# Hats of three taps fetched in one set of transfers, with one ScalarE copy for the three and a ring of twelve

## The chip, the core and the metric

The kernel runs on one core of a Trainium2 chip (trn2). Its time is the device time of one execution in microseconds, the median of several; less is better. The five engines of the core each walk a list of instructions in order: TensorE (PE), VectorE (DVE), ScalarE (ACT), GpSimd (POOL) and SyncE (SP, which here only issues DMAs). They wait for one another by semaphores.

## What is computed

The input is 16 images of 64 channels and 16x16 pixels, in f32. Four layers follow one another:

```python
x = x + softmax(q @ k.T / 8) @ v                   # L0: attention over channels (64x64)
om = conv3x3(x, w_off) + b_off                     # L1: offsets (18) and mask (9) for each pixel
sampled[k] = bilinear(x, py[k], px[k]) * sigmoid(mask[k])      # k: 9 taps
x = relu(batchnorm(sum_k w_dcn[k] @ sampled[k] + b_dcn))
x = x + wp @ attention_over_pixels(q2, k2, v2)     # L2: 256x256 softmax for each image
y = depthwise3x3(layernorm(x))                     # L3
x = x + fuse @ sum_of_4_scans(conv5(y) * sigmoid(gate @ y))
x = x + ff2 @ (a * sigmoid(g)), [a, g] = ff1 @ layernorm(x)
```

## The kernel before

Two images stand side by side on the 128 partitions, so there are 8 pairs. Every engine walks its own list of PLAN (lines 56 to 127): an entry `step.n` is one step of pair n, and in PE's list `@m0` and the like name the PSUM bank (m0 to m2, or the double banks p0, p1 of `quad`). `turn` makes a PE step wait until the step that held its bank before is done. Nothing is ordered at run time: what stands behind a waiting instruction of an engine waits too.

**The hats.** Bilinear sampling is done by matmuls. The weight of a source pixel (y, x) for an output pixel is the product of two hats, one for each axis: max(0, 1 - |distance|), the hat of y times the mask. For each pair, `dist` (L847, DVE) gives the distances of each output pixel's position from the 16 rows and 16 columns, for 9 taps; `abs` (L678, ACT) and `hat` (L852, DVE) make the hats of them in the tile `hat` [128, 4, 18, 16]; `tanh` (L671, ACT) gives the mask, and `hat_y` (L860, DVE, scalar_tensor_tensor) multiplies (mask + 1) onto the y hats. PE transposes them in three groups of three taps, `tr0` to `tr2` (L467), ACT copies each out of PSUM (L686, 96 rows of 512), and `put` (L693, ACT's queue) writes them to `hat_rows` in HBM. A tap has 32 rows there, 16 of y and 16 of x, each of 2 KB (two images, 256 output pixels).

**The ring.** `get` (L333, L336, SP) reads a tap back with three DMAs: `xe`, 64 partitions of 2 KB (a row of x each, repeated for 4 runs), and two halves of `wt`, 64 partitions of 4 KB each (two rows of y, repeated for 16 columns). So one DMA moves 128 KB, two 256 KB. There is a ring of nine slots, RING = 9; a get waits until the sample nine taps back is done (`smp_mm`). ACT copies `xe` from partitions 0-63 to 64-127 (`d0` to `d8`, L712), DVE multiplies it into `wt` (`w0` to `w8`, L868, 128x1024), and PE samples (`s0` to `s8`, L497): four matmuls of the logical size 128x256 against `w_x`, all nine taps of a pair into the bank `cv`. `relu` (L719) takes the sum of nine taps out as x2. `w_x` are the images times the layer's weights (`wx0` to `wx2`, L482 and L703).

**Behind the samples.** qk2, logit, max (L875, L878), exp (L741), nrm (L888), et (L547, L750), av (L559), x3; then st1, ln1 (POOL: L1009 to L1018, five small steps; ACT: L757), dw (L762, L764, L910), y (L918), gs (gates and scans, L571 and L579, which need all four banks of quad), gate and scan (L774, L781), prod (L924), fuse (L589), x4 (L932), st2, ln2 (again POOL's five steps), ff (L601), u (L944), ff2 (L610), out (L951), store.

**Filler.** `warm` (L375) and `hot` (L381) are matmuls on a tile of zeros whose result nothing reads; one round is two matmuls of the program. WARM and HOT give the rounds of each entry. In the profile a matmul of f32 data appears as two; those of the filler as one.

## Time and profile before

| | us |
|---|---|
| median of 3 runs | 281.18 (280.73 to 282.88) |
| the profiled execution | 282.63 |
| its span in the profile | 280.8 |
| PE busy in it | 252.6 (90%) |
| DVE busy | 204.7 (73%) |
| ACT busy | 184.1 (66%) |
| POOL busy | 53.3 (19%) |
| DMA packets, bytes | 22881, 56.47 MB |

Times of instructions are from the profiled execution alone. An engine's share of busy time is an average over stages with different limits: the front, in which the first pairs' offsets are computed, the long middle in which 72 taps pass through the ring, and the tail behind the last sample, in which the last pairs' other layers end. "Idle before" tells how long an engine stood still ahead of a group of instructions and which instruction ended that. The DMA share can be a little above 1, as the durations of packets overlap.

### The profile page before, as it was taken

Reading aid. Unit: us, or ns where it says so; the run is one execution under the profiler, and the core shown is the slowest. Engines: PE = TensorE matmul, PEld = TensorE weight load, DVE = VectorE, ACT = ScalarE, POOL = GpSimd, SP = SyncE. Lnnn points to the kernel's source line nnn. Section 1 sums busy time; section 2 is a strip of 40 time slices with the busy share of each in tenths; the row PEclk is TensorE's granted clock in tenths of the full one; section 3 lists DMA queues with packets and bytes.
Section 4 is the critical chain, followed back from the end, with each engine's and each line's share of the span. In section 5 each row is a group of like instructions: output and inputs, shape, how many; then the busy total and the mean of one; then the engine's idle time right before and its main releaser. Section 6 shows DMA issues by size and latency. Waiting matters only on the chain.

```text
span 280.8 us, 7247 instructions
## 1 busy us (share of the span) xinstructions
PE 252.6 (90%) x2796; PEld 167.5 (60%) x2796; DVE 204.7 (73%) x353; ACT 184.1 (66%) x391; POOL 53.3 (19%) x99
## 2 busy tenths in 40 slices
...
GB/s 233 204 0 176 242 284 272 322 245 287 280 294 270 240 297 267 241 304 281 258 259 251 248 247 268 268 283 253 244 259 256 110 19 22 2 2 0 9 30 19
DMA packets 22881, 56.47 MB, mean 201 GB/s; under 512 B 4160, under 2 KB 6464, under 8 KB 22720
## 3 DMA queue, kind: packets, MB, share of 16 engines
...
## 4 chain that ended last, share of the span: by engine, by line
PE 51%; DVE 17%; ACT 13%; issue 9%; POOL 8%; ACTq 0%; DVEq 0%; POOLq 0%
PE ps_cv L497 11%; PE ps_quad L579 5%; PE ps_quad L482 5%; PE ps_m L444 5%; DVE sb_wt L868 5%; POOL sb_sc L1012 2%; PE ps_quad L571 2%; PE ps_m L467 2%; PE ps_quad L601 2%; ACT sb_xe L712 2%; PE ps_m L559 2%; DVE sb_b_max L875 2%; PE ps_m L511 2%; ACT sb_gates L774 2%; PE ps_quad L536 2%
## 5 line engine op out<-in xcount | busy, mean ns | idle before, releaser
L868 DVE TENSOR_TENSOR sb_wt<-sb_wt,sb_xe 128x1024 f32<-128x1024 f32 x72 | 87.9, 1233 | 11.7 <-ACT sb_xe L712 11.5
L497 PE MATMUL ps_cv<-sb_wt,sb_w_x 128*64 128x256 f32 x576 | 74.9, 388 | 5.3 <-DVE sb_wt L868 4.4
L497 PEld LDWEIGHTS ps_cv<-sb_wt,sb_w_x 128*64 128x64 f32 x576 | 40.2, 138 | 27.5 <-DVE sb_wt L868 7.9
L712 ACT ACTIVATE sb_xe<-sb_xe 64x512 f32<-64x512 f32 x72 | 44.8, 627 | 3.4 <-ACT sb_hats L686 1.6
L1009 POOL TENSOR_SCALAR sb_sc<-sb_mv 128x1 f32<-128x1 f32 x16 | 9.8, 612 | 116.6 <-DVE sb_mv L940 64.1
L910 DVE SCALAR_TENSOR_TENSOR sb_dw_acc<-sb_z_pad,sb_par,sb_dw_acc 128x256 f32<-128x256 f32 x56 | 23.0, 479 | 6.8 <-ACT sb_dw_acc L762 6.8
L482 PE MATMUL ps_quad<-sb_par,sb_x 64*128 64x256 f32 (+1 forms) x192 | 24.3, 378 | 0.8 <-ACT sb_w_x L703 0.6
L1002 POOL COPY sb_x<-sb_x_pad 128x256 f32<-128x256 f32 x8 | 6.3, 787 | 92.6 <-PE ps_quad L482 57.4
L774 ACT ACTIVATE sb_gates<-ps_quad,sb_gate_bh 128x512 f32<-128x512 f32 x16 | 10.1, 681 | 17.0 <-PE ps_quad L579 17.0
L703 ACT ACTIVATE sb_w_x<-ps_quad 128x1024 f32<-128x1024 f32 (+1 forms) x24 | 19.0, 807 | 3.0 <-PE ps_quad L482 1.8
L482 PEld LDWEIGHTS ps_quad<-sb_par,sb_x 64*128 64x128 f32 x192 | 16.7, 197 | 6.8 <-issue 5.7
L579 PE MATMUL ps_quad<-sb_y_pad,sb_par 32*64 32x256 f32 x640 | 20.4, 383 | 0.3 <-issue 0.3
L847 DVE TENSOR_TENSOR sb_dist<-ps_m,sb_grid 128x1152 f32<-128x1152 f32 x8 | 10.8, 1355 | 11.8 <-PE ps_m L455 11.8
L741 ACT ACTIVATE sb_b_exp<-ps_quad,sb_b_neg 128x256 f32<-128x256 f32 x32 | 14.8, 471 | 5.1 <-DVE sb_b_neg L878 4.8
L381 PE MATMUL ps_cv<-sb_idle 128*64 128x512 f16 x144 | 17.9, 396 | 0.0
L444 PE MATMUL ps_m<-sb_x_pad,sb_par 128*64 128x128 f32 x288 | 17.5, 272 | 0.4 <-DVE sb_x_pad L838 0.4
L579 PEld LDWEIGHTS ps_quad<-sb_y_pad,sb_par 32*64 32x64 f32 x640 | 14.0, 129 | 5.7 <-issue 3.4
L444 PEld LDWEIGHTS ps_m<-sb_x_pad,sb_par 128*64 128x64 f32 x288 | 16.4, 136 | 0.9 <-DVE sb_x_pad L838 0.4
L686 ACT ACTIVATE sb_hats<-ps_m 96x512 f32<-96x512 f32 x24 | 13.6, 590 | 5.2 <-PE ps_m L467 4.4
L467 PE MATMUL ps_m<-sb_par,sb_hat 128*96 128x128 f32 x96 | 13.9, 279 | 1.9 <-ACT sb_hats L686 1.4
L1012 POOL TENSOR_TENSOR sb_sc<-sb_sc,sb_half 128x1 f32<-128x1 f32 x16 | 14.4, 897 | 1.3
L467 PEld LDWEIGHTS ps_m<-sb_par,sb_hat 128*96 128x96 f32 x96 | 9.7, 126 | 7.7 <-issue 6.5
...
## 6 DMA issues: line engine op xcount, KB each, us to landing
sb_wt<-hat_rows SPq DMA_DIRECT2D x144, 256.0 KB, 10.3
...
```

Source lines behind the costliest of these rows:

```text
L381: nc.tensor.matmul(cv[columns_of(t), :], idle[:, columns_of(t)], idle[:, :], start=True, stop=True)
L444: mm = nc.tensor.matmul(ma[C * h:C * (h + 1), 0:P], par_sb[:, a + 2 * OM * t:a + 2 * OM * (t + 1)], x1_pad[n % 2][:, r:r + HALF_ROWS, t % ...
L467: mm = nc.tensor.transpose(ma[0:ROWS, at:at + P], hat[:, 2 * h + b, axes, :], ident)
L482: mm = nc.tensor.matmul(pair[:, 512 * b + PIX * h:512 * b + PIX * h + k], x1[n % 2][r, 2 * h:2 * (h + 1), :, :], par_sb[r, a:a + k], start ...
L497: mm = nc.tensor.matmul(cv[C * b:C * (b + 1), 0:PIX], w_x[n % 2][:, b, h, k, :], wt[slot(n, k)][:, h, PIX * b:PIX * (b + 1)], start=(k == ...
L579: mm = nc.tensor.matmul(quad[columns_of(d), 512 * i:512 * i + PIX], par_sb[r, a:a + C], rows, start=(j == 0), stop=(j == KS - 1))
L703: nc.scalar.activation(w_x[n % 2][:, :, :, t0:t1, :].rearrange("p b h t c -> p b h (t c)"), held(f"wx{c}", n)[:, :].rearrange("p (b h q) - ...
L712: nc.scalar.activation(xe[i][C:P, :], xe[i][0:C, :], ACT.Copy).then_inc(ev("dup_ok"), 1)
L774: last = nc.scalar.activation(gates[:, s, :, :], of_half(1, s), ACT.Tanh, bias=gate_bh[:, s:s + 1], scale=0.5)
L868: nc.vector.tensor_tensor(wt[i][:, :, :], wt[i][:, :, :], xe[i][:, :].unsqueeze(1).to_broadcast([P, HALVES, 2 * PIX]), ALU.mult)\
L910: nc.vector.scalar_tensor_tensor(out=sum_of, in0=dw_source(t), scalar=col("dw_w", t), in1=sum_of, op0=ALU.mult, op1=ALU.add).then_inc(ev(f ...
L1012: nc.gpsimd.tensor_tensor(scl[:, 1:2], scl[:, 0:1], half[:, :], ALU.pow).then_inc(ev(rstd_ok), 1)
```

## The change

1. The hats lie in another order: for each group of three taps, axis by axis, with the three taps innermost (`hat` is [128, 4, 3, 2, 48]). `abs` writes this order, the transposes read it without a step. In HBM a row of x or y now has its three taps side by side.
2. A get fetches a group: one DMA of 64 partitions x 6 KB (384 KB) and two of 64 x 12 KB (768 KB each). The ring has 4 slots of three taps; a get waits until all three samples of the group four back are done. The products of a group wait for both halves and for one ACT copy of 64x1536.
3. mask + 1 is computed by a new step `msk` on POOL, between `tanh` (ACT) and `hat_y` (DVE), which becomes a tensor_tensor.
4. The maximum of the softmax comes out negated (`negate=True`), the scale is put into q2; the step with -QK_SCALE is gone.
5. The two norms have four POOL steps in place of five; their gains with both signs are computed once, by four steps at the start.
6. Four buffers go (b_nrm, prod, ff_u, b_max), their results are written in place, with waits for the readers of the pair or two pairs before.
7. The lists of all engines are written anew, with other banks; HOT has 10 entries of 48 rounds in all (before 8 of 72), WARM 5 entries of 18 (before 6 of 18).

The core of the diff:

```diff
-RING = 9
+SLOTS = 4
...
     "pe": """
...
-        s4.8 v2.7@m1 et0.7@m2 s5.8 s6.8 s7.8 ff2.5@m2 s8.8 et1.7@m1 qk2.8@m2 av.7@m1 v2.8@m0 logit.8@p0 hot.1 et0.8@m1
-        gs.6@p0+p1 et1.8@m1 hot.2 av.8@m1 gs.7@p0+p1 fuse.6@m1 hot.3 fuse.7@m1 ff.6@p1 hot.4 gs.8@p0+p1 ff2.6@m1 hot.5
-        ff.7@p0 fuse.8@m1 hot.6 ff2.7@m1 hot.7 ff.8@p0 hot.8 ff2.8@m1
...
+        v2.7@m1 s1.8 gs.5@p0+p1 s2.8 fuse.4@m0 s3.8 s4.8 s5.8 ff.3@p0 logit.7@p1 s6.8 s7.8 s8.8 ff2.3@m0 fuse.5@m1
+        qk2.8@m2 et0.7@m0 ff.4@p1 logit.8@p0 et1.7@m0 v2.8@m1 av.7@m0 ff2.4@m1 hot.1 ff.5@p1 et0.8@m1 hot.2 et1.8@m0
+        hot.3 ff2.5@m1 av.8@m0 gs.6@p0+p1 hot.4 gs.7@p0+p1 fuse.6@m0 hot.5 gs.8@p0+p1 fuse.7@m0 hot.6 ff.6@p0 fuse.8@m0
+        hot.7 ff2.6@m1 ff.7@p0 hot.8 ff2.7@m0 hot.9 ff.8@p0 hot.10 ff2.8@m0
...
-HOT = {1: 15, 2: 5, 3: 11, 4: 9, 5: 10, 6: 4, 7: 10, 8: 8}
-WARM = {1: 5, 2: 3, 3: 3, 4: 2, 5: 3, 6: 2}
+HOT = {1: 2, 2: 2, 3: 1, 4: 10, 5: 6, 6: 6, 7: 3, 8: 8, 9: 2, 10: 8}
+WARM = {1: 5, 2: 3, 3: 3, 4: 2, 5: 5}
...
-        xe = [sb(f"xe{i}", [P, 2 * PIX]) for i in range(RING)]
-        wt = [sb(f"wt{i}", [P, HALVES, 2 * PIX]) for i in range(RING)]
+        xe = [sb(f"xe{i}", [P, OF_GROUP, 2 * PIX]) for i in range(SLOTS)]
+        wt = [sb(f"wt{i}", [P, HALVES, OF_GROUP, 2 * PIX]) for i in range(SLOTS)]
...
+            def get(g):
+                def step(n):
+                    sp.wait_ge(rows_out[n % 2][g], 16 * ((n + 1) // 2))
+                    wait_past(sp, ev("smp_mm"), OF_GROUP * (group(n, g) - SLOTS))
+                    i = slot(n, g)
+                    sp.dma_start(xe[i][0:C, :, :].rearrange("p t q -> p (t q)"),
+                                 rows[n - 1, g, ROWS // 2:ROWS, :].rearrange("(x t) q -> x (t q)", t=OF_GROUP).unsqueeze(1)
+                                 .to_broadcast([W, RUN, OF_GROUP * 2 * PIX])).then_inc(slot_x[i], 16)
                     for j in range(2):
...
+                        a = ROWS // 4 * j
+                        sp.dma_start(wt[i][C * j:C * (j + 1), :, :, :].rearrange("p h t q -> p (h t q)"),
+                                     rows[n - 1, g, a:a + ROWS // 4, :].rearrange("(y k) q -> y (k q)", y=RUN).unsqueeze(0)
+                                     .to_broadcast([W, RUN, HALVES * OF_GROUP * 2 * PIX])).then_inc(slot_in[i], 16)
...
+                nc.scalar.activation(hat[:, :, :, :, :].rearrange("p j g a (i t) -> p (j g) t (a i)", t=OF_GROUP),
+                                     dist[:, :, :, :].rearrange("p j (g t a) i -> p (j g) t (a i)", t=OF_GROUP, a=2), ACT.Abs)\
                     .then_inc(ev("abs_ok"), 1)
...
+            def dup(g):
+                def step(n):
+                    i = slot(n, g)
+                    act.wait_ge(slot_x[i], filled(n, g))
+                    nc.scalar.activation(xe[i][C:P, :, :], xe[i][0:C, :, :], ACT.Copy).then_inc(ev("dup_ok"), 1)
...
+                of_y = hat[:, :, :, 0, :].rearrange("p j g (i t) -> p (j g) i t", t=OF_GROUP)
+                mask = msk1[:, :, :].rearrange("p j (g t) -> p (j g) t", t=OF_GROUP).unsqueeze(2)                    .to_broadcast([P, 4 * GROUPS, H, OF_GROUP])
+                nc.vector.tensor_tensor(of_y, of_y, mask, ALU.mult)\
                     .then_inc(ev("hat_y_ok"), 1)
...
+                    g, t = divmod(k, OF_GROUP)
+                    i = slot(n, g)
+                    dve.wait_ge(slot_in[i], 2 * filled(n, g))
+                    dve.wait_ge(ev("dup_ok"), group(n, g))
+                    nc.vector.tensor_tensor(wt[i][:, :, t, :], wt[i][:, :, t, :],
+                                            xe[i][:, t, :].unsqueeze(1).to_broadcast([P, HALVES, 2 * PIX]), ALU.mult)                        .then_inc(ev("wt_ok"), 1)
...
-                dve.wait_ge(ev("max_ok"), n)
-                nc.vector.tensor_scalar(b_neg[n % 2][:, :], b_max[n % 2][:, :], -QK_SCALE, None, ALU.mult).then_inc(ev("neg_ok"), 1)
+                wait_past(dve, ev("exp_ok1"), n - 2)
+                nc.vector.tensor_reduce(b_neg[n % 2][:, :], held("logit", n)[:, :].rearrange("p (i j) -> p i j", j=PIX), AX_X, ALU.max,
+                                        negate=True).then_inc(ev("neg_ok"), 1)
...
+            def msk_step(n):
+                pool.wait_ge(ev("tanh_ok"), n)
+                wait_past(pool, ev("hat_y_ok"), n - 1)
+                nc.gpsimd.tensor_scalar(msk1[:, :, :], msk[:, :, :], 1.0, 1.0, ALU.add, ALU.mult).then_inc(ev("msk_ok"), 1)
```

## Rows read from the trace of the kernel before

**Rows 1.** The page, busy time (share of the span) and instructions of each engine

```profile
PE 252.6 (90%) x2796; PEld 167.5 (60%) x2796; DVE 204.7 (73%) x353; ACT 184.1 (66%) x391; POOL 53.3 (19%) x99
```

**Rows 2.** groups of instructions: the filler. busy us, mean ns | idle before us

```profile
L381 PE MATMUL ps_cv<-sb_idle 128*64 128x512 f16 x144 | 17.9, 396 | 0.0
...
L375 PE MATMUL ps_cv<-sb_idle 128*64 128x512 f16 x36 | 6.5, 450 | 1.2 <-DVE sb_idle L962 1.2
```

**Rows 3.** stretches: window, length, busy us of each engine, clock, DMA share, GB/s

```profile
5.00:10.00 5.00, 4.12 (x52) 2.79 (x48) 3.00 (x7) 0.73 (x4) 2.15 (x1) 1.00 1.02 376
30.00:219.00 189.00, 170.45 (x1880) 116.62 (x1876) 155.11 (x244) 138.06 (x287) 34.59 (x52) 0.98 1.04 267
219.00:231.20 12.20, 12.20 (x108) 7.72 (x106) 11.16 (x20) 9.77 (x22) 4.33 (x8) 1.00 0.14 46
231.20:280.80 49.60, 43.04 (x522) 24.12 (x520) 24.59 (x56) 21.51 (x44) 8.68 (x25) 0.96 0.04 12
```

**Rows 4.** timeline: start, duration of the first and last product and last sample

```profile
36.29 1.22 DVE L868 TENSOR_TENSOR sb_wt<-sb_wt,sb_xe 128x1024 f32<-128x1024 f32 x1
...
228.46 1.22 DVE L868 TENSOR_TENSOR sb_wt<-sb_wt,sb_xe 128x1024 f32<-128x1024 f32 x1
...
230.18 1.03 PE L497 MATMUL ps_cv<-sb_wt,sb_w_x 128*64 128x256 f32 x8
```

**Rows 5.** waits of SP's queue: us in total, times, longest

```profile
SPq L333 <- PE ps_cv L497: 27.6, 18, 3.1
SPq L304 <- PE ps_cv L497: 17.2, 10, 4.3
```

**Rows 6.** the page, DMA issues: KB each, median us to landing

```profile
sb_wt<-hat_rows SPq DMA_DIRECT2D x144, 256.0 KB, 10.3
```

**Rows 7.** waits of the compute engines: us in total, times, longest

```profile
DVE sb_wt L868 <- ACT sb_xe L712: 11.5, 11, 2.1
...
PEld ps_cv L497 <- DVE sb_wt L868: 7.9, 11, 2.4
```

**Rows 8.** groups of instructions: the copy, a longer ScalarE pass, the product

```profile
L868 DVE TENSOR_TENSOR sb_wt<-sb_wt,sb_xe 128x1024 f32<-128x1024 f32 x72 | 87.9, 1233 | 11.7 <-ACT sb_xe L712 11.5
...
L712 ACT ACTIVATE sb_xe<-sb_xe 64x512 f32<-64x512 f32 x72 | 44.8, 627 | 3.4 <-ACT sb_hats L686 1.6 <-issue 0.3
...
L678 ACT ACTIVATE sb_hat<-sb_dist 128x1152 f32<-128x1152 f32 x8 | 9.3, 1160 | 0.0
```

**Rows 9.** groups of instructions: the PE steps that move

```profile
L589 PE MATMUL ps_m<-sb_prod,sb_fuse_h 128*64 128x256 f32 x64 | 8.6, 390 | 0.6 <-DVE sb_prod L924 0.5
...
L601 PE MATMUL ps_quad<-sb_z,sb_par 64*128 64x256 f32 x64 | 9.7, 424 | 3.0 <-ACT sb_z L786 1.3 <-ACT sb_w_x L703 1.3 <-ACT sb_conv L781 0.4
...
L610 PE MATMUL ps_m<-sb_ff_u,sb_ff_h 128*64 128x256 f32 x32 | 5.1, 398 | 0.6 <-DVE sb_ff_u L944 0.6
```

**Rows 10.** timeline of the start, pair 1: abs, hat, first get

```profile
17.46 1.16 ACT L678 ACTIVATE sb_hat<-sb_dist 128x1152 f32<-128x1152 f32 x1
...
18.65 0.76 DVE L852 TENSOR_SCALAR sb_hat<-sb_hat 128x1152 f32<-128x1152 f32 x1 [1.32 <-ACT sb_hat L678]
...
23.67 0.61 SPq L333 DMA_DIRECT2D sb_xe<-hat_rows  x1
```

**Rows 11.** timeline of GpSimd: short steps, and one beside DVE's product

```profile
219.98 0.19 POOL L1016 TENSOR_TENSOR sb_sc<-sb_mv,sb_sc 128x1 f32<-128x1 f32 x1
220.25 0.19 POOL L1018 TENSOR_TENSOR sb_sc<-sb_par,sb_sc 128x1 f32<-128x1 f32 x1
226.89 1.10 POOL L1009 TENSOR_SCALAR sb_sc<-sb_mv 128x1 f32<-128x1 f32 x1 [6.45 <-DVE sb_mv L904]
```

**Rows 12.** timeline of the tail: negation, pair 8's y, its scans

```profile
237.19 0.17 DVE L878 TENSOR_SCALAR sb_b_neg<-sb_b_max 128x4 f32<-128x4 f32 x1
...
257.11 0.41 DVE L918 TENSOR_TENSOR sb_y_pad<-sb_dw_acc 128x256 f32<-128x256 f32 x1
...
261.11 0.74 PEld L571 LDWEIGHTS ps_quad<-sb_y_pad,sb_par 64*128 64x128 f32 x8 [0.41 <-issue]
```

More of the change, by code:

```diff
@@ L96 @@
-        ff.6 gate.8 ln2.7 scan.8 ff.7 ln2.8 ff.8
+        attn.1 at.1 mix.1 attn.2 attn.3 at.2 halve.1 off.1 prep.1 mix.2 abs.1 tanh.1 wx0.1 wx1.1 tr0.1 tr1.1 put0.1
+        tr2.1 wx0.2 put2.1 put1.1 off.2 at.3 attn.4 mix.3 tanh.2 abs.2 wx1.2 at.4 wx2.1 off.3 tr2.2 tr0.2 put0.2 put2.2
+        tanh.3 tr1.2 put1.2 mix.4 abs.3 d0.1 attn.5 off.4 d1.1 tr1.3 put1.3 at.5 tanh.4 tr0.3 put0.3 mix.5 d2.1 tr2.3
+        put2.3 abs.4 off.5 attn.6 relu.1 wx0.3 d0.2 q2.1 k2.1 wx2.2 wx1.3 tr2.4 put2.4 attn.7 tanh.5 d1.2 v2.1 exp0.1
@@ new lines @@
+        exp1.1 tr1.4 tr0.4 et0.1 wx2.3 put0.4 et1.1 put1.4 d2.2 at.6 abs.5 mix.6 at.7 ln1.1 dw.1 mix.7 d0.3 tr0.5 relu.2
+        put0.5 wx0.4 off.6 wx2.4 q2.2 k2.2 d1.3 v2.2 tanh.6 exp0.2 exp1.2 tr1.5 abs.6 put1.5 tr2.5 et0.2 d2.3 et1.2
+        put2.5 wx1.4 d0.4 tr2.6 ln1.2 relu.3 wx0.5 tr0.6 dw.2 tr1.6 q2.3 k2.3 v2.3 d1.4 put2.6 put0.6 put1.6 exp0.3
+        off.7 exp1.3 attn.8 d2.4 et1.3 et0.3 wx1.5 abs.7 tanh.7 at.8 d0.5 mix.8 relu.4 wx0.6 wx1.6 q2.4 k2.4 d1.5 gate.1
+        ln1.3 scan.1 dw.3 tr1.7 tr0.7 put0.7 tr2.7 d2.5 gate.2 put2.7 scan.2 put1.7 v2.4 off.8 d0.6 ln2.1 exp0.4 wx2.5
@@ L113 @@
-        x4.8 u.7 st2.8 out.7 u.8 out.8
+        qk.1 a_max.1 a_norm.1 qk.2 qk.3 a_max.2 a_max.3 a_norm.2 x1.1 a_norm.3 dist.1 qk.4 hat.1 hat_y.1 x1.2 a_max.4
+        dist.2 a_norm.4 x1.3 hat.2 hat_y.2 dist.3 qk.5 qk.6 hat.3 a_max.5 hat_y.3 x1.4 w0.1 a_norm.5 w1.1 qk.7 w2.1
+        dist.4 w3.1 w4.1 w5.1 x1.5 w6.1 w7.1 a_max.6 w8.1 a_norm.6 hat.4 qk.8 hat_y.4 dist.5 a_max.7 w0.2 w1.2 w2.2
+        max.1 a_norm.7 w3.2 w4.2 nrm0.1 nrm1.1 w5.2 x3.1 st1.1 w6.2 hat.5 w7.2 hat_y.5 w8.2 dw2.1 x1.6 dw4.1 w0.3 dw6.1
```

223 lines of the change are left out of this document (95 added, 128 removed).

## The prediction

> **What bounds the kernel now.** I read the busy times first. TensorE (PE) is busy 252.6 of 280.8 us, VectorE (DVE) 204.7, ScalarE (ACT) 184.1 [rows 1]. Part of PE's time is filler: 144 idle matmuls of "hot" (17.9 us) and 36 of "warm" (6.5 us) [rows 2], so the real PE work is 252.6 - 24.4 = 228.2 us, and about 52 us of the span are filler or gaps.
>
> Then I cut the span where the work changes its kind [rows 3]. From 30 to 219 us the DMA engines never rest (share 1.04) and PE is busy 170.45 of 189 us. From 219 on the gets are done, but sampling goes on: the last product of hats starts on DVE at 228.46 and the last sampling matmuls on PE at 230.18 [rows 4]. The last get had landed some 8 to 9 us earlier: from 219 to 231.2 the share is 0.14 of 12.2 us, 1.7 us of full work, so the stream ends near 220 [rows 3]. After 231.2 the tail of 49.6 us holds 43.04 us of PE, of which 17.9 are filler (all of hot stands behind sample 8.8 in the list): 25.1 us of real work [rows 2, 3]. So the end is set by two things: when sample 8.8 is done (231.2), and how long the chain of pair 8 is behind it.
>
> Is the middle bound by DMA? Its share says full, and SyncE (SP) waits 27.6 + 17.2 = 44.8 us in all for slots that sampling has not freed [rows 5]. A get lands a median of 10.3 us after its issue [rows 6], while a round of the ring of nine takes nine times (231.2 - 36.3) / 72 = 2.7 us, 24 us [rows 4]. So data lies ready for some 10 us before it is used, DMA is full but ahead, and the list of waits has no row of an engine that waited for a get to land. What the sampling does wait for is ACT's copy (11.5 us, 11 times), and PE's weight loads for DVE's product (7.9 us) [rows 7]. These are waits in an order written by hand: the engines (PE, DVE, ACT) are 90%, 82% and 73% busy in this stretch [rows 3], and each step stands behind others of its own engine.
>
> **The change, part by part.**
>
> *Transfers.* 216 gets become 72, of the same 46 MB (384 KB and two of 768 KB for each group). SP had 44.8 us to wait for slots [rows 5], so it was not the bound, and a third of the issues is worth nothing. The rate: gets with rows of 2 and 4 KB run at 267 GB/s at a share of 1.04; the loads at 5 to 10 us, with rows of 1 to 9.6 KB, at 376 at 1.02 [rows 3]. Rows of 6 and 12 KB are so bounded between 267 and 376. I take 267, since the gets read each row 16 times over and the loads do not; then a group lands 1.92 MB / 267 = 7.2 us after the one before. At 376 it would be 5.1. With the stream full as it is now, the last get lands near 219.5, or earlier at a better rate; behind it stand one copy of 1.48 (below), three products of 1.23 [rows 8] and the last sample of 1.03 [rows 4], so sampling can't end before 219.5 + 6.2 = 225.7 at the old rate.
>
> The Trainium skill (DMA: Bandwidth & Descriptors, "Why small descriptors are slow") says that joining descriptors is worth it only at 256 B and less. By that rule rows of 6 and 12 KB get no rate over those of 2 and 4 KB, the stream stays at 267 GB/s, and the rival of a faster stream (below) falls away. The trace does not decide it: 376 against 267 is also unique rows against repeated ones.
>
> *ScalarE.* 72 copies of 627 ns become 24. From 512 to 1152 elements a ScalarE pass grows by (1160 - 627) / 640 = 0.83 ns an element [rows 8], so 1536 elements cost 627 + 1024 x 0.83 = 1.48 us. 44.8 us become 35.5: 9.3 us less ACT. Little of it is on the path, as ACT is 73% busy; it serves the 11.5 us of DVE's waits, which I leave in the order's gain below [rows 7]. Against it, at the end, the last three products wait for a copy of 1.48 in place of 0.63: +0.85 us.
>
> *The order of work.* I compared the two lists on either side of sample 8.8. On PE these steps move from ahead of it to behind it: ff2.3, ff2.4, ff2.5, fuse.5, ff.4, ff.5, et0.7; none moves the other way. From the rows: ff2 5.1 / 8 = 0.64 each, fuse 8.6 / 8 = 1.08, ff 9.7 / 8 = 1.21 each [rows 9]; et0 is four matmuls of 128 columns, an estimate of 0.6 from half of fuse's. In sum 1.92 + 1.08 + 2.42 + 0.6 = 6.0 us. On DVE ten steps move likewise (prod.5, max.7, x4.5, st2.5, u.3 to u.5, out.3, out.4, nrm0.7), several microseconds, as prod.5 and max.7 alone each pass over as many elements as a product of 1.23 [rows 8]. Both engines that could hold sampling back are relieved, so sample 8.8 ends 6.0 us earlier, at 225.2, which the landing bound above (225.8) nearly allows. What moves behind must be taken up there: "hot" falls from 72 to 48 rounds, 48 matmuls of 17.9 / 144 = 0.124 us [rows 2] = 6.0 us less filler. The tail keeps its length and its filling. Bounds of this term: 0 (the middle keeps its end and only idles more) to -11.5 in place of -6.0, where the copy waits of rows 7 go too, all of them. I take -6.0.
>
> *The start.* The first gets go out at 23.67 [rows 10] behind the hats of pair 1. "hat_y" now waits for a new step on GpSimd (POOL), mask + 1, between ACT's tanh and DVE. Queued behind waiting hat_y on DVE are w's and x1 steps; queued behind msk on POOL are x1 (sampling weights) and the two norms. Its price is between 0.19 us, the shortest POOL row, and 1.10, the same kind beside a DVE product [rows 11]. In pair 1, abs comes before tanh: abs ends at 18.6, tanh at 18.8, msk at about 19.1, when DVE's own hat pass (18.65 to 19.41) still runs [rows 10]; so at most 0.2 is seen. In pairs 2 to 8 the hats are needed many microseconds later, hidden by the ring; without this cover it would be 8 x 0.19 to 8 x 1.10. I take +0.2. Four gain steps and one ScalarE scale at the start lie before 17 us beside PE work: nothing. PE's s0.1 comes behind mix.4, qk.7, x1.4 and off.4, the same work in another order: nothing.
>
> The first use: group 1 lands whole about 23.7 + 10.3 = 34.0 (7.2 of bytes, 3 of the way; the median landing of now, an estimate from rows 6), and w0.1 ran only at 36.29 [rows 4], with more ahead of it now: nothing.
>
> *Short steps of the last chain.* The softmax's negation (0.17 and a gap of 0.02 us) [rows 12] goes into the reduction; each norm loses one POOL step, 0.19 and 0.08 to the next [rows 11]: 0.19 + 2 x 0.27 = -0.73 us on pair 8. Elsewhere covered. Reusing buffers in place adds waits (exp on et of two pairs before, scan on fuse, ff on ff2 of the pair before); the PE list has each of those ahead of need, nothing, and up to 1.1 us (one fuse) where gs.7 precedes fuse.6.
>
> *The wait before the last scan.* Pair 8's y is written at 257.11 + 0.41 = 257.5, but gs.8 begins at 261.11 [rows 12], as ff.6 and the 18 idle matmuls of hot.4 stand ahead of it in PE's list. Now gs.8 has 12 idle matmuls before it and the PE work that moved back fills in. Between 0 and -3.6; I take -2.0.
>
> **Sum.** -6.0 + 0.85 + 0.2 - 0.73 - 2.0 = -7.7 us. Of the profiled execution (span 280.8, its time 282.63) this makes 273.1 and 274.9; that execution stood 1.45 above the median of 281.18, so the forecast is 281.18 - 7.7 = 273.5 us.
>
> **Rivals.**
>
> 1. *A faster stream.* Rows of 6 and 12 KB go at 350 GB/s or so and ACT's spare time takes DVE's waits away: of the 18.5 us in which PE idles from 30 to 219, a third (6 us) goes too. For it: 376 GB/s of the loads. Against: the data already waits 10 us. Time: 273.5 - 6 = 267.5.
>
> 2. *The middle does not shorten.* PE's gaps there belong to chains of softmax and norms over four engines, and work taken from PE leaves only wider gaps. For it: the waits of rows 7 are small and many, and none is a transfer. Against: PE is busy 12.2 of the last 12.2 us of sampling [rows 3]. Then -0.73 and 0.5 of the last wait remain: 280.
>
> 3. *Whole-group landing, the slower side.* A slot comes free only after its third sample and its data is of use only when all 1.92 MB are there, copied in one pass. With PE's order fixed, a stall at the first sample of each group pushes everything behind it. A landing takes some 10.3 us and a round of four groups 32, less 8 of use, so 13 us are spare, which speaks against it. For it: each put of hats must now be ready three taps sooner. If each of the 24 groups stalls 0.5 us: 281.2 - 7.7 + 12 = 285.5. It decides (slower than now) from 7.7 / 24 = 0.32 us a group.
>
> The Trainium skill (GPSIMD Engine Reference, "Key points") adds that GpSimd contends with VectorE instructions of two SBUF inputs, which each product is; that the new POOL step stretches from 0.19 to over 1 us is its case, and the trace agrees [rows 11].
>
> **Numbers.** Forecast 0.5 (its own range 270 to 278), rival 1 0.17, rival 2 0.20, rival 3 0.13. The range 267 to 282.5 reaches from rival 1 past rival 2. Three runs of the kernel before spread by 0.8%, so about 1% is what a measurement tells from no change. Faster by over 1% (below 278.4): rival 1 and nearly all of the forecast, 0.66; within 1%: rival 2 and edges, 0.20; slower 0.14.
>
> **What would show it.** Right: copies of 64x1536 at 1.48 us, ACT near 175 us busy; hot at 96 matmuls and 12 us; last sampling matmuls ending at 225 +/- 2; a tail of 46 to 48 us; gs.8 less than 2 us after y.8; gets at 267 to 300 GB/s. Wrong: sampling ending at 230 (rival 2), sampling rows of PE or DVE waiting for a get (rival 3), a share of DMA below 0.9 between 40 and 210 with an early end (rival 1).

## The result, and the profile after

The changed kernel takes 299.79 us (median of 4 runs, 296.0 to 304.55) against 281.06 (280.73 to 282.88, 4 runs). The ratio is 1.0531, with a 95% interval of 1.0451 to 1.0611: slower by 5%, where 273.5 us was forecast and 267 to 282.5 given as the range. The profiled execution took 302.85 us with a span of 301.1; it and one more of the four stood higher at a lower clock and are left out of the ratio, as such executions are from every ratio below, and the other two took 296.0 and 296.73, so of the 20.3 us that are followed below through the profiled span some 6 belong to that execution.

Busy times, and the issues of DMAs (KB each, median us from issue to landing) of the kernel after:

```profile
PE 257.0 (85%) x2748; PEld 169.6 (56%) x2748; DVE 202.2 (67%) x345; ACT 178.9 (59%) x344; POOL 50.9 (17%) x95
...
sb_wt<-hat_rows SPq DMA_DIRECT2D x48, 768.0 KB, 21.8
sb_xe<-hat_rows SPq DMA_DIRECT2D x24, 384.0 KB, 17.8
hat_rows<-sb_hats ACTq DMA_DIRECT2D x24, 192.0 KB, 12.8
```

No engine has much more to do than before [rows 1], and the span is 20.3 us longer: the engines wait. What for is in the list of waits (us in total, times, longest), first of the compute engines:

```profile
DVE sb_wt L869 <- DMA sb_wt<-hat_rows: 42.5, 18, 4.4
...
PE ps_cv L493 <- DVE sb_wt L869: 15.8, 13, 3.6
```

The row that did not exist before [rows 7] is now the longest of them for DVE: the product waits for the hats themselves, 42.5 us in all. Then of SP's queue:

```profile
SPq L301 <- PE ps_cv L493: 113.4, 17, 13.0
...
SPq L328 <- DMA hat_rows<-sb_hats: 55.2, 7, 16.9
```

SP waits 113.4 us for slots, against 44.8 before [rows 5], although the data then comes too late: the slots that sampling does not hold are issued already and not landed. A median landing of 21.8 us, where it was 10.3 [rows 6], is the same thing seen from the transfer. Puts wait among the long gets too (12.8 us, 7.8 before), and SP waits 55.2 us for them (16.9 before); low_first below has the loss without either. Stretches of the kernel after (length, busy us of each engine, clock, DMA share, GB/s):

```profile
35.00:238.00 203.00, 167.87 (x1696) 111.92 (x1697) 143.14 (x219) 123.19 (x223) 23.63 (x38) 0.92 1.02 239
...
255.00:301.00 46.00, 41.15 (x512) 23.81 (x508) 28.56 (x67) 25.69 (x52) 11.65 (x24) 0.99 0.06 19
```

Here is the loss. The DMA engines are as full as before (share 1.02) but move 239 GB/s where they moved 267 [rows 3]. Gets and puts are 47.2 + 4.7 = 51.9 MB, and 51.9 / 0.239 - 51.9 / 0.267 = 23 us. So much later the stream ends: DMA falls silent near 243, before near 220. The chain that ended last (start, us) shows it; gets of the y-hats are 38% of it, and the chain of the kernel before has none:

```profile
56.23 17.27 DMA sb_wt<-hat_rows
73.52 1.24 DVE sb_wt L869
...
85.03 24.74 DMA sb_wt<-hat_rows
...
117.15 29.11 DMA sb_wt<-hat_rows
...
160.51 22.33 DMA sb_wt<-hat_rows
...
197.97 20.83 DMA sb_wt<-hat_rows
218.82 1.23 DVE sb_wt L869
```

(PE's mean granted clock is 0.92 in this stretch, with PE busy for 83% of it, and was 0.98 with 90% [rows 3]. What the lower clock costs is not priced here.) The last product and the last sampling matmuls:

```profile
249.95 1.23 DVE L869 TENSOR_TENSOR sb_wt<-sb_wt,sb_xe 128x1024 f32<-128x1024 f32 x1
...
252.19 2.81 PE L493 MATMUL ps_cv<-sb_wt,sb_w_x 128*64 128x256 f32 x24
```

Sampling ends at 255.0 instead of 231.2 [rows 4], +23.8; the tail is 46.1 us instead of 49.6 [rows 3], -3.5; together +20.3, the whole difference of the spans. Two groups bear on the forecast: ScalarE's new copy came out as forecast, its abs did not.

```profile
L709 ACT ACTIVATE sb_xe<-sb_xe 64x1536 f32<-64x1536 f32 x24 | 35.6, 1483 | 8.5 <-DMA sb_xe<-hat_rows 8.0
...
L675 ACT ACTIVATE sb_hat<-sb_dist 128x1152 f32<-128x1152 f32 x8 | 14.4, 1801 | 4.5 <-DVE sb_dist L847 3.9
```

So the question for the experiments is: why do the same bytes, by fewer and larger transfers, move at 239 GB/s?

### The profile page after: what moved, and what is told of

Read it like the earlier page. It is cut to its first block, busy times and chain, and to the rows that moved or that the text cites. A ratio compares the mean times of both kernels' runs of the same rounds, so it can differ in the third digit from the quotient of the medians.

```text
span 301.1 us, 6980 instructions
## 1 busy us (share of the span) xinstructions
PE 257.0 (85%) x2748; PEld 169.6 (56%) x2748; DVE 202.2 (67%) x345; ACT 178.9 (59%) x344; POOL 50.9 (17%) x95
## 4 chain that ended last, share of the span: by engine, by line
DMA 44%; PE 36%; DVE 7%; ACT 5%; issue 3%; SPq 2%; POOL 2%; ACTq 0%; POOLq 0%; DVEq 0%
DMA sb_wt<-hat_rows 38%; PE ps_cv L493 8%; DMA hat_rows<-sb_hats 6%; PE ps_quad L575 6%; PE ps_quad L567 3%; DVE sb_wt L869 2%; PE ps_m L463 2%; PE ps_quad L597 2%; PE ps_quad L478 2%; PE ps_m L543 2%; PE ps_cv L372 2%; PE ps_m L441 1%; ACT sb_conv L780 1%; PE ps_m L555 1%; PE ps_m L387 1%
## 5 line engine op out<-in xcount | busy, mean ns | idle before, releaser
L869 DVE TENSOR_TENSOR sb_wt<-sb_wt,sb_xe 128x1024 f32<-128x1024 f32 x72 | 87.9, 1232 | 42.5 <-DMA sb_wt<-hat_rows 42.5
L493 PE MATMUL ps_cv<-sb_wt,sb_w_x 128*64 128x256 f32 x576 | 76.6, 401 | 17.9 <-DVE sb_wt L869 15.8
L493 PEld LDWEIGHTS ps_cv<-sb_wt,sb_w_x 128*64 128x64 f32 x576 | 41.5, 142 | 42.2 <-issue 15.7
L709 ACT ACTIVATE sb_xe<-sb_xe 64x1536 f32<-64x1536 f32 x24 | 35.6, 1483 | 8.5 <-DMA sb_xe<-hat_rows 8.0
L1022 POOL TENSOR_SCALAR sb_sc<-sb_mv 128x1 f32<-128x1 f32 x16 | 8.3, 522 | 119.9 <-DVE sb_mv L940 89.4
L910 DVE SCALAR_TENSOR_TENSOR sb_dw_acc<-sb_z_pad,sb_par,sb_dw_acc 128x256 f32<-128x256 f32 x56 | 24.3, 477 | 1.5 <-ACT sb_dw_acc L761 1.4
L700 ACT ACTIVATE sb_w_x<-ps_quad 128x1024 f32<-128x1024 f32 (+1 forms) x24 | 18.9, 808 | 1.5 <-PE ps_quad L478 1.0
L675 ACT ACTIVATE sb_hat<-sb_dist 128x1152 f32<-128x1152 f32 x8 | 14.4, 1801 | 4.5 <-DVE sb_dist L847 3.9
L463 PEld LDWEIGHTS ps_m<-sb_par,sb_hat 128*96 128x96 f32 x96 | 10.6, 133 | 11.1 <-issue 9.3
L1016 POOL TENSOR_SCALAR sb_msk<-sb_msk 128x36 f32<-128x36 f32 x8 | 3.6, 449 | 72.7 <-ACT sb_msk L668 72.7
L876 DVE TENSOR_REDUCE sb_b_neg<-ps_quad 128x4 f32<-128x1024 f32 x8 | 9.8, 1221 | 7.0 <-PE ps_quad L532 7.0
## 6 DMA issues: line engine op xcount, KB each, us to landing
sb_wt<-hat_rows SPq DMA_DIRECT2D x48, 768.0 KB, 21.8
hat_rows<-sb_hats ACTq DMA_DIRECT2D x24, 192.0 KB, 12.8
```

The source lines that it names most:

```text
L463: mm = nc.tensor.transpose(ma[0:ROWS, at:at + P], hat[:, 2 * h + b, g, :, :], ident)
L493: mm = nc.tensor.matmul(cv[C * b:C * (b + 1), 0:PIX], w_x[n % 2][:, b, h, k, :], wt[slot(n, k // OF_GROUP)][:, h, k % OF_GROUP, PIX * b:PI ...
L675: nc.scalar.activation(hat[:, :, :, :, :].rearrange("p j g a (i t) -> p (j g) t (a i)", t=OF_GROUP), dist[:, :, :, :].rearrange("p j (g t ...
L700: nc.scalar.activation(w_x[n % 2][:, :, :, t0:t1, :].rearrange("p b h t c -> p b h (t c)"), held(f"wx{c}", n)[:, :].rearrange("p (b h q) - ...
L709: nc.scalar.activation(xe[i][C:P, :, :], xe[i][0:C, :, :], ACT.Copy).then_inc(ev("dup_ok"), 1)
L869: nc.vector.tensor_tensor(wt[i][:, :, t, :], wt[i][:, :, t, :], xe[i][:, t, :].unsqueeze(1).to_broadcast([P, HALVES, 2 * PIX]), ALU.mult) ...
```

## The experiments

Fifteen kernels ran, two of them twice. The letters of theories are each text's own; A2 is the one that first stands in stream4. Where the computation is left out, the times say nothing of the kernel; only the GB/s of the stretches are read.

### Which part of the change: order_before, rows4k, tapgets

**order_before** keeps the change's transfers and takes the lists and filler of before.

```diff
-    (the changed PLAN, HOT and WARM)
+    (those of the kernel before; get and copy of a group where its first tap's stood, msk behind bn.1 and x1)
```

> The changed kernel with the lists and the filler of the kernel before (the copy of a group where its first tap's stood, the mask step put in behind the sampling copies of GpSimd). Theory A and B: still 295 or more, as the transfers are the new ones. Theory C (the new order is the fault): back to 281 to 285.

302.43 us, ratio 1.0752 (1.0702 to 1.0802). The loss is there with the old order. The y-hats land in 19.9 us, puts in 13.3.

**rows4k** keeps all of the changed kernel, its HBM layout and its one semaphore for a group, but cuts the three transfers into nine, with rows of 2 and 4 KB, and the y-hats for partitions 0 to 63 and 64 to 127 in turn.

```diff
-                    for j in range(2):
+                    for c in range(3):
+                        for j in range(2):
...
-                        sp.dma_start(wt[i][C * j:C * (j + 1), :, :, :].rearrange("p h t q -> p (h t q)"),
+                        sp.dma_start(wt[i][C * j:C * (j + 1), :, :, :].rearrange("p h t q -> p (h t q)")[:, 4 * PIX * c:4 * PIX * (c + 1)],
```

> The changed kernel, with each group's three DMAs cut into nine of 2 and 4 KB rows, same slots, same semaphores for the whole group. Theory A (row length sets the rate, and the rate the time): the stream returns to 260 GB/s or more, the puts of hats land in 8 us instead of 13, the time falls to 283 to 288. Theory B (the landing of whole groups and the order cost the time): no change, 294 to 300, as a group still lands as one.

278.84 us, ratio 0.9895 (0.984 to 0.995). That alone takes away 21 us of the median, 17 to 18 from the two lower executions of the changed kernel.

**tapgets** keeps the changed order, the ring of twelve and the one copy for three taps; hat layout, transfers, their semaphores and the release tap by tap are those of before.

```diff
-        hat = sb("hat", [P, 4, GROUPS, 2, H * OF_GROUP])
+        hat = sb("hat", [P, 4, AXES, H])
...
+                    for t in range(OF_GROUP):
+                        wait_past(sp, ev("smp_mm"), OF_GROUP * (group(n, g) - 1 - SLOTS) + t + 1)
```

> The changed kernel with its new order and ring of twelve, but the hats' layout and the transfers of the kernel before: by tap, rows of 2 and 4 KB, a semaphore and a release for each tap; one ScalarE copy for three taps stays. Theory A: as rows4k, 280 to 286. Theory B (whole-group landing): clearly below rows4k, 272 to 278. Theory C (the new order is bad by itself): stays at 290 or more.

275.93 us (271.16 to 276.53), too spread for an interval. The same kernel in another run:

> The kernel with a transfer for each tap, hat layout of before, one copy for three taps, ring of twelve and the changed order, timed again in more rounds: 275.9 us, so 0.975 to 0.985 of the kernel before. If the order and the copy bring nothing by themselves: 0.99 to 1.01.

273.65 us, ratio 0.976 (0.970 to 0.9819). This is the version that beats both. What it has of the change is worth -2.4%; the loss lies in what it leaves out.

### Row length, or where the rows go: stream, stream2, low_first, wide

**stream** is SyncE alone, with the ring's waits, in five forms of eight groups (15.7 MB each).

> All computation is left out: SyncE alone fills the four slots, in five forms of 8 groups (15.7 MB) one after another, four slots deep: (1) by tap, repeated rows of 2 and 4 KB as in the kernel before; (2) by group, repeated rows of 6 and 12 KB as in the changed kernel; (3) by group from the new layout but cut to rows of 2 and 4 KB; (4) rows of 6 and 12 KB, each read once only; (5) rows of 2 and 4 KB, each read once. Theory A (long repeated rows are slower in themselves): form 1 near 267 GB/s, 59 us; form 2 near 239, 66 us; form 3 like form 1. Theory B (the rate falls only beside the computation or by the order of the work): forms 1, 2 and 3 within 2% of each other. If repetition of rows is what costs, forms 4 and 5 go at 350 GB/s or more, 45 us.

The stretches of the five forms (length, busy POOL, clock, DMA share, GB/s): by tap as before; by group as changed; the group's layout in rows of 2 and 4 KB with the halves in turn; every partition a row of its own, 6 and 12 KB; own rows of 2 and 4 KB, the halves in blocks.

```profile
30.00:90.00 60.00, 0.00 (x0) 1.00 1.05 232
102.00:166.00 64.00, 0.00 (x0) 1.00 1.02 213
176.00:238.00 62.00, 0.00 (x0) 1.00 1.04 239
248.00:310.00 62.00, 0.00 (x0) 1.00 1.01 212
326.00:388.00 62.00, 0.00 (x0) 1.00 1.05 210
```

The loss shows without any computation: 213 against 232. Reading a row sixteen times costs nothing (213 and 212). The fifth form is the surprise: short rows, and as slow as long ones. What it shares with the slow forms is that many bytes in a row go to one half of the partitions. So theory A, row length, does not hold as it stands.

Every form is slower than the same pattern in a whole kernel: 232 against 267 [rows 3], 213 against 239, 239 against 270 of rows4k. The kernels also have puts from a second queue among the gets; no run shows whether that is the reason. Only differences within the streams are read here.

**stream2** fills y-hat tiles only: low half alone, 4 KB rows; low half alone, 12 KB; 4 KB, low and high in turn; 4 KB, three low and three high; 128 partitions in one transfer, 4 KB; the same, 12 KB.

> All computation is left out: SyncE fills only the tiles of the y hats, four slots deep, in six forms one after another. Every DMA reads repeated rows. (1) partitions 0 to 63 only, rows of 4 KB; (2) partitions 0 to 63 only, rows of 12 KB (11 MB each); then 15.7 MB each: (3) rows of 4 KB, one DMA to partitions 0-63 and one to 64-127 in turn; (4) the same DMAs, three to 0-63 and then three to 64-127; (5) rows of 4 KB, each DMA to all 128 partitions (partition = 8 x column + row); (6) the same with rows of 12 KB. Theory A (long rows are slow): forms 2 and 6 slower than 1 and 5. Theory D (64 partitions are half of the ways into SBUF, so that a stream in which long stretches go to one half runs at half speed, and small DMAs to alternate halves overlap): forms 1, 2 and 4 all at 205 to 220 GB/s whatever the row, form 3 above 240, forms 5 and 6 at 350 or more and equal.

```profile
30.00:72.00 42.00, 0.00 (x0) 1.00 1.04 214
84.00:130.00 46.00, 0.00 (x0) 1.00 1.02 205
140.00:196.00 56.00, 0.00 (x0) 1.00 1.04 245
204.00:268.00 64.00, 0.00 (x0) 1.00 1.04 226
276.00:340.00 64.00, 0.00 (x0) 1.00 1.04 233
348.00:396.00 48.00, 0.00 (x0) 1.00 1.01 215
```

One half alone is limited to 214, in turn it is 245, in blocks 226. Rows of 12 KB cost 4 to 8% against 4 KB. But 128 partitions at once reached 233 and 215 and not the 376 of the loads [rows 3]: "half of the partitions, half of the rate" is not the whole cause.

**low_first** puts this to the real kernel. It is rows4k with its two loops exchanged, so the same transfers, rows and semaphores, in another order.

```diff
-                    for c in range(3):
-                        for j in range(2):
+                    for j in range(2):
+                        for c in range(3):
```

> As rows4k (rows of 2 and 4 KB, 279 us), but the six DMAs of the y hats go out as three to partitions 0-63 and then three to 64-127, in place of in turn. Theory A (row length): no change, 277 to 281. Theory D (halves): the stream falls back to 239 GB/s or so and the time to 290 to 300, though the rows are short.

303.36 us, ratio 1.083 (1.076 to 1.0901), against 0.9895 of rows4k. From 60 to 205 us, first of rows4k and then of low_first:

```profile
60.00:205.00 145.00, 126.66 (x1322) 84.74 (x1324) 114.69 (x177) 103.42 (x191) 25.65 (x37) 0.98 1.04 270
```

```profile
60.00:205.00 145.00, 120.54 (x1136) 80.55 (x1132) 102.39 (x157) 91.47 (x168) 18.83 (x29) 0.91 1.04 237
```

And its longest wait of DVE:

```profile
DVE sb_wt L871 <- DMA sb_wt<-hat_rows: 40.8, 15, 4.4
```

The rate is that of theory D (239 GB/s or so) and the time a little above its 290 to 300 us. Nothing but the order of the halves is worth 24.5 us, and it brings back the rate (237) and the wait (40.8) of the changed kernel. Its puts land in 8.9 us, and SP waits 20.8 us for them, so the slow puts of the changed kernel are not what costs it. This is the decisive run among the whole kernels.

**wide** fills 128 partitions with each transfer (partition = 8 x column + row) and has no ScalarE copy; x-hats are moved twice, 20% more bytes.

```diff
-                        sp.dma_start(xe[i][0:C, t, :], rows[n - 1, g, a + H:a + 2 * H, :].unsqueeze(1)
+                        sp.dma_start(xe[i][:, t, :], rows[n - 1, g, a + H:a + 2 * H, :].unsqueeze(1)
```

> The changed kernel's order and ring of twelve, with another placing of source pixels on partitions (partition = 8 x column + row): a tap is two DMAs, each to all 128 partitions, 512 KB of y hats in rows of 4 KB and 256 KB of x hats in rows of 2 KB, a semaphore for each tap, and no ScalarE copy at all (20% more bytes from HBM, 56.6 MB). Theory D: the gets run at 340 GB/s or more, sampling no longer waits for them, and with 35 us less of ScalarE work the time is 268 to 274. Theory A (rows of 4 KB run at 267 whatever the partitions): 56.6 MB need 212 us, the time is 285 or more.

302.25 us, ratio 1.0684 (1.056 to 1.0808): theory D, with 340 GB/s and 268 to 274 us, missed. It ran at 288 GB/s from 60 to 205 us, 8% above the 267 of the kernel before, for gets of 20% more bytes.

### How the sixteen engines meet: stream3, stream4, stream5

**stream3**, 4 KB rows throughout.

> Computation left out: SyncE alone fills the y-hat tiles from HBM, 4 KB rows throughout, 15.7 MB in each of six forms. Forms 1 and 2: every partition reads a row of its own, in transfers to all 128 partitions (512 KB), then to the halves in turn (256 KB). Forms 3 and 4: one row goes to eight (four) neighbouring partitions, so the sixteen engines read different rows at a moment. Forms 5 and 6: the kernel's y pattern, where all sixteen engines read the same rows. Theory A (what limits is the side that writes into SBUF, by how many of its ways are open at once): the source makes no difference; forms 1, 3, 5 are alike, forms 2, 4, 6 near 245 GB/s as in the second stream run. Theory B (besides, engines that read one and the same row of HBM at once stand in each other's way): forms 5 and 6 stay at 231 and 245, forms 1 and 3 reach 300 or more, as the loads at the kernel's start do, and forms 2 and 4 lie between. Rival C (short transfers cost by themselves): the forms with 512 KB are faster than those with 256 KB whatever the halves.

```profile
28.00:58.00 30.00, 0.00 (x0) 1.00 1.02 406
75.00:125.00 50.00, 0.00 (x0) 1.00 1.04 229
145.00:195.00 50.00, 0.00 (x0) 1.00 1.04 234
215.00:265.00 50.00, 0.00 (x0) 1.00 1.04 239
285.00:335.00 50.00, 0.00 (x0) 1.00 1.04 235
355.00:405.00 50.00, 0.00 (x0) 1.00 1.04 244
```

Neither theory fits: own rows to 128 partitions run at 406, own rows to halves at 229, and at 128 partitions it drops to 234 as soon as eight neighbouring partitions share a row. Form 3 has different rows for each engine, so several engines reading one row at once is not it. What also differs between forms 1 and 3 is how a transfer falls into sixteen parts: form 3 is a pattern of 16 x 8, so if its sixteen runs go to the sixteen engines, each engine has eight neighbouring partitions.

The Trainium skill (SBUF — State Buffer, "Door 1: The DMA port swizzle") says that 16 ports lead into SBUF, eight of them for partitions 0 to 63 and eight for 64 to 127, and that partitions 32 apart share one. The Trainium skill (DMA: Bandwidth & Descriptors, "The descriptor swizzle") adds that a plain transfer to 128 partitions is divided so that each engine has a port of its own. By these, sixteen engines with four or eight neighbouring partitions each stand two to a port at any moment if they keep step, and 64 partitions starting at 32 would give each of them its own. The next run puts both to the test.

**stream4**, five forms: own rows in sixteen runs of eight with gaps between; 128 partitions that all read one row; the y pattern to partitions 32 to 95; to 0 to 31 and 96 to 127 in turn; a tap in a new division.

> Computation left out: SyncE alone fills the y-hat tiles, 4 KB rows, five forms in turn. Form 1 (15.7 MB): 128 partitions, every partition a row of its own, but the rows lie as 16 runs of eight with gaps, so that the transfer is cut into sixteen runs of eight neighbouring partitions. Form 2 (15.7 MB): 128 partitions that all read one and the same row. Form 3 (15.7 MB): the kernel's y pattern, into partitions 32 to 95. Form 4 (15.7 MB): the y pattern into partitions 0 to 31 and 96 to 127 in turn, 128 KB each. Form 5 (23.6 MB): a tap's share in a new division: x-hats into 0 to 63 (128 KB), y-hats into 32 to 95 (256 KB), into 0 to 31 and into 96 to 127 (128 KB each). Theory A2 (what decides is how the sixteen engines fall on the ways into SBUF at one moment, not what is read): form 1 falls from 409 to about 235 although it reads no row twice, form 2 reaches about 409 although all read one row, form 3 reaches 300 to 400 although it fills only 64 partitions, form 4 stays at 240 or below, form 5 lies between, 270 or more. Theory B (rows read several times over are slow in HBM): form 1 is 409, form 2 is slowest of all, form 3 is 210 to 245 like the other y patterns.

```profile
35.00:85.00 50.00, 0.00 (x0) 1.00 1.04 245
105.00:130.00 25.00, 0.00 (x0) 1.00 1.03 410
150.00:170.00 20.00, 0.00 (x0) 1.00 1.03 409
190.00:255.00 65.00, 0.00 (x0) 1.00 0.50 187
310.00:360.00 50.00, 0.00 (x0) 1.00 0.78 245
```

Two rows decide between the theories. Own rows fall from 406 to 245 when the pattern is 16 x 8 (their runs now also lie with gaps between them in HBM); and the y pattern, at 214 into partitions 0 to 63, runs at 409 into partitions 32 to 95, with rows of the same size. How often a row is read does not matter (410 with one row for all). What matters is which partitions a transfer fills and in what division, and both rows come out as the ports have it. A transfer of 8 x 4 to 32 partitions has a DMA share of 0.50: half of the engines work. Form 5 was forecast at 270 or more and ran at 245.

**middle** brings this into a real kernel. In tapgets the pixels of columns 0 to 7 change sides, so that one transfer for each tap goes to 32 to 95.

```diff
-                        for j in range(2):
-                            sp.dma_start(wt[i][C * j:C * (j + 1), t, :, :].rearrange("p h q -> p (h q)"),
+                        for p, q, j in ((32, 96, 0), (0, 32, 1), (96, P, 1)):
+                            sp.dma_start(wt[i][p:q, t, :, :].rearrange("p h q -> p (h q)"),
```

> The kernel with the changed one's order and ring, the hat layout of before and one ScalarE copy for three taps (275.9 us), with one thing more: the pixels of columns 0 to 7 change sides, so that the y-hats of rows 0 to 3 of each half image go to partitions 32 to 95 in one transfer, and the others to 0 to 31 and 96 to 127. Bytes are the same, one transfer more for each tap (384 for 288 in all ... 72 taps by 4), and GpSimd copies the image in three parts. Theory A2: the stream runs at 270 GB/s or more where it ran at 240 undisturbed, so 184 us of stream become at most 165 and the kernel takes 255 to 270 us. Theory B, or a stream bound by the number of transfers: 276 us or more.

286.07 us, ratio 1.0117 (1.0011 to 1.0223), where theory A2 had 255 to 270 us (a tap has four transfers for three, 288 in all for 216). The DMA share is 0.79 and the rate 256 from 60 to 205 us: the two small transfers have half of the engines each. What is gained on partitions 32 to 95 is lost on 0 to 31 and 96 to 127, as in form 5 of stream4, 245.

**stream5** leaves the transfers as they are and tries to change only the engines' step. Eight partitions give work to eight of the sixteen engines, so a small transfer of that kind in front should put these behind the others.

> Computation left out: SyncE fills the y-hat tiles with the kernel's y pattern, 4 KB rows. Form 1 (18.9 MB): low and high half in turn, 256 KB each. Form 2 (18.9 MB): the same behind one small transfer that only engines 0 to 7 carry out (eight partitions of 16 KB), so that these eight are one transfer behind the other eight. Form 3 (23.6 MB): a tap's share as in the kernel before (x-hats low 128 KB, y-hats low, y-hats high 256 KB each). Form 4: form 3 behind such a transfer of eight partitions of 20 KB. Form 5 (18.9 MB): the low transfers from SyncE's queue, the high ones from ScalarE's at the same time. If the sixteen engines go in step and so meet on the same ways into SBUF (theory A2), then forms 1 and 3 run at about 245 and 230 GB/s, form 2 at up to 410 as long as the lag lasts, form 4 at 280 or more, and form 5 between 245 and 410. If they do not go in step, forms 2 and 4 are like 1 and 3 (within 3%), and the 410 of the transfers to partitions 32 to 95 needs another reason.

```profile
35.00:95.00 60.00, 0.00 (x0) 1.00 1.04 241
116.00:170.00 54.00, 0.00 (x0) 1.00 1.04 286
190.00:270.00 80.00, 0.00 (x0) 1.00 1.05 234
295.00:360.00 65.00, 0.00 (x0) 1.00 1.05 284
380.00:425.00 45.00, 0.00 (x0) 1.00 1.04 313
```

One transfer of 128 KB in front, by eight engines only, lifts the 18.9 MB behind it from 241 to 286, and one of 160 KB the tap's pattern from 234 to 284, with no decline up to the end of either form. Two queues side by side give 313. This fits engines that go in step, at a price. It is short of the 410 of transfers without that price, no profile shows where an engine stands, and no run put a transfer of all sixteen engines in front for comparison, so the step itself is argued and its effect measured.

### The lag in the real kernels

One transfer more on SP, ahead of the first get (or of each pair's):

```diff
+                    if g == 0 and n == 1:
+                        sp.dma_start(spare[:, :], x.rearrange("n p q -> (n p) q")[0:8 * 80, :]
+                                     .rearrange("(p k) q -> p (k q)", k=80)).then_inc(lag, 16)
```

> The changed kernel with one transfer more, ahead of the first get: eight rows of 80 KB from HBM to a spare place in HBM, which engines 0 to 7 alone carry out, so that they are some 3 us behind the other eight, about half of a group's time. Theory A2 (engines in step meet on half of the ways into SBUF): where the stream ran at 212 to 226 GB/s undisturbed it now runs at 250 or more, as long as the lag lasts; if it lasts to the end, the time falls from 299.8 to 265 to 285 us; if the stream loses it at its first pause, the time stays within 3 us of 300 and only the first windows are faster. If the step of the engines has no part in it: 300 to 303 us throughout.

302.89 us, ratio 1.0794 (1.0707 to 1.0881), 241 GB/s from 60 to 205 us. Nothing came of it. SP waits for the second put until 34 us, ten us after the lag was sent at 24.5, and the DMA share is 0.61 from 27 to 30 us; whether the engines meet again there was not shown. The test says nothing for or against.

> The same transfer ahead of each pair's first get, eight in all (5.2 MB more on engines 0 to 7 alone, 24 us of their time in all, if it weren't hidden). Theory A2: where one lag is lost after a pause the next makes a new one, but one that comes while the lag still stands moves it by another 3 us and may undo it; 270 to 295 us. Without such a mechanism eight engines have 8 x 3 us more to do and the kernel takes 310 us or more.

311.76 us, ratio 1.1025 (1.0893 to 1.1158), as without the mechanism, or with lags that undo one another; not told apart.

> The kernel with a transfer for each tap, hat layout of before, one copy for three taps and the changed one's order (275.9 us), with one transfer of eight rows of 32 KB ahead of the first get, by engines 0 to 7 alone. Theory A2: its 240 GB/s become 270 to 285 as long as the lag lasts; 255 to 272 us if it lasts past the middle. Without: 275 to 277 us.

275.57 us (271.2 to 277.41). From 60 to 150 and 150 to 205 us, first of tapgets and then of tap_lag:

```profile
60.00:150.00 90.00, 78.28 (x825) 53.15 (x825) 71.03 (x108) 61.91 (x119) 12.78 (x18) 0.96 1.04 269
150.00:205.00 55.00, 48.21 (x491) 32.40 (x491) 46.64 (x71) 39.21 (x76) 11.10 (x19) 1.00 1.03 280
```

```profile
60.00:150.00 90.00, 78.81 (x846) 54.24 (x846) 72.52 (x114) 62.75 (x119) 17.69 (x18) 0.96 1.04 300
150.00:205.00 55.00, 52.68 (x588) 35.44 (x586) 48.99 (x77) 41.44 (x78) 12.46 (x19) 1.00 1.00 252
```

That looks like a success of the lag: 300 in place of 269 for 90 us, and a span of 269.4 in place of 273.6. But tapgets' second run, without any lag, has this in the same stretches, with a span of 270.0:

```profile
60.00:150.00 90.00, 79.54 (x812) 54.51 (x811) 70.23 (x107) 61.21 (x118) 18.09 (x18) 0.92 1.04 287
150.00:205.00 55.00, 53.57 (x612) 36.36 (x607) 50.33 (x79) 41.66 (x80) 12.14 (x19) 1.00 1.00 267
```

So 18 of the 31 GB/s come and go without a lag. From 60 to 205 us, tapgets has 273 and 279 GB/s in its two runs, the kernel with the lag 282 and 276 (in its second run, below). The lowest executions are 271.2 us with it and 271.2 without. The lag is not shown to work in a whole kernel, and neither is the step of the engines. (The 240 GB/s of the expectation is tapgets' rate only at the end of its stream, 239 from 190 to 205 us.)

> The same with the lag made anew ahead of each pair (2.1 MB more on engines 0 to 7). Theory A2: 255 to 272 us. Without: 278 us or more.

277.86 us, ratio 0.9693 (0.9604 to 0.9781, from its two lower executions, 272.3 and 272.4); no better than the kernel without. The kernel with one lag again, beside tapgets:

> The same with the one lagging transfer, timed beside it on the same chip. Its trace had 288 to 325 GB/s between 68 and 150 us and 240 after. If a faster middle of the stream shortens the kernel: 2 us or more below the run beside it; if PE and the last pairs' chains decide by then: within 1 us of it.

276.96 us (271.33 to 282.16), beside 273.65 (271.66 to 276.47) of tapgets: not faster.

## Why the prediction was wrong

**The step that failed** is the first term, "Rows of 6 and 12 KB are so bounded between 267 and 376. I take 267". It stands in the sum as nothing. The bounds were drawn by row length, and the reason for the choice was that the gets "read each row 16 times over". Both were beside the point: repeated reading costs nothing (213 and 212), longer rows cost 4 to 8% in one stream (stream2) and nothing in another (210 and 212), and what the loads at 376 have and the gets have not is the division of a plain transfer over 128 partitions. The lower end of the bound excluded a loss for no reason. The term measured 239 GB/s, +23 us on 51.9 MB of the profiled execution: sampling ended at 255.0, where the sum has about 226 (225.2 + 0.85 + 0.2). Its cause: 384 KB and 768 KB to partitions 0 to 63, then 768 KB to 64 to 127, where the kernel before changed sides every 256 to 384 KB. Long stretches to one side are slow, frequent changes faster (stream: 213, 232, 239; whole kernels: low_first 237, rows4k 270). In whole kernels this is shown by the exchange of two loops. Why it is so, sixteen engines on half of the ways into SBUF, is argued from streams without computation (214 and 409 by the partitions, 241 and 286 by the transfer in front) and not shown in a whole kernel.

**"So data lies ready for some 10 us" and "13 us are spare"** failed with it. The 10.3 us of landing were taken as a fixed delay. They are what a queue would give, by an estimate: 10.3 us x 267 GB/s = 2.75 MB, four taps of 0.655 MB ahead of each. With a slower stream the queue grows (21.8 us x 239 = 5.2 MB), SP's wait for slots grows with it (113.4 us), and no spare is left. A DMA share of 1.04 over 189 us should have weighed more than SP's 44.8 us of waiting: both engines and DMA were near their limit, and a loss of 10% in either was bound to show in full.

**Rival 3** had the right place and sign (DVE waiting for a get to land), and its deciding point, 0.32 us a group, was passed by far: 42.5 / 24 = 1.8 us. But it saw the cause in the landing as a whole, and that costs less: rows4k lands by group as well and takes 278.84, some 3 to 5 us above tapgets, with the slower abs (below) among them. Rival 1, the faster stream, was wrong.

**What held.** The changed kernel without its transfers and their hat layout is tapgets: 0.976 of 280.22, -6.7 us (-5.1 to -8.4), where the sum without any effect of the stream was -7.7 us. So the order, the copy and the tail together were sized about right for a kernel that lands tap by tap: its sampling ends at 227.6 and 223.9 in its two profiled executions, where the sum has about 226 and the kernel before 231.2. With landing by group and the slower abs it is otherwise. rows4k, all of the change but the cut of its transfers, gains 1% (-2.9 us): its sampling ends at 232.3, so nothing is left of the -6.0 ahead of sample 8.8, and DVE waits 20.8 us for gets. Its tail of 46.0 us is its whole gain. In detail: the copy 1483 ns (1.48 forecast); hot 96 matmuls of 12.2 us; a tail of 46.1 us (46 to 48), the same within 0.1 in tapgets and rows4k; and pair 8's last scan now begins right behind its y (us; y written, then the scan's matmuls):

```profile
278.88 0.42 DVE L918 TENSOR_TENSOR sb_y_pad<-sb_dw_acc 128x256 f32<-128x256 f32 x1
...
280.10 1.15 PE L567 MATMUL ps_quad<-sb_y_pad,sb_par 64*128 64x256 f32 x8 [0.37 <-ACT sb_conv L780]
```

0.8 us lie between them, 3.6 before [rows 12]: -2.8 where -2.0 was taken. PE and DVE relieved ahead of sample 8.8 could not show in the changed kernel, as transfers set its middle; in tapgets it does.

**Missed:** abs now writes its result with a stride and takes 1801 ns in place of 1160 [rows 8], 8 x 0.64 = 5.1 us of ScalarE, 0.64 of it ahead of the first get, which went out at 24.18 after 23.67. No run priced it by itself in the time. With it ScalarE's 178.9 us stand above the forecast 175. "The first use: nothing" missed too: the first product starts at 41.4 us and not at 36.29 [rows 4]. In order_before it starts at 37.3 and in tapgets at 39.8, so the greater part of this came with the new order. And a group is 1.97 MB, which at 267 GB/s is 7.4 us and not 7.2; nothing hangs on that.
